# The half q too much in VectorE's rows of an L1-distance attention: taken off through sums of q, or by row matmuls on q itself

## The reference, cut to what matters

```python
def one_query(qs):
    return -jnp.sum(jnp.abs(qs[:, None, :, :] - k), axis=-1) * scale   # scale = 1/sqrt(64)
...
v = (x @ wqv_w.T + wqv_b).reshape(b, t, 3 * h, d)
q, vf, vb = (v[:, :, :h], v[:, :, h:2 * h], v[:, :, 2 * h:])
k = x[:, :, None, :] * wk[None, None]
a = _l1_scores(q, k)
a = jnp.concatenate([a, jnp.zeros((b, 1, t, h), a.dtype)], axis=1)
a = jax.nn.softmax(a, axis=1)[:, :t]
bf = jnp.einsum('bsdh,bshw->bdhw', a, vf)
bb = jnp.einsum('bdsh,bshw->bdhw', a, vb)
o = (bf + bb).sum(axis=2).reshape(b, t, d)
```

## Time and profile before

| | us |
|---|---|
| three runs: median (lowest to highest) | 9558.85 (9547.97 to 9571.28) |
| the profiled execution, its own time | 9557.57 |
| its span, first to last instruction | 9555.7 |
| TensorE matmuls busy | 9349.8 (98%) |
| ScalarE busy | 7738.5 (81%) |
| VectorE busy | 7116.6 (74%) |
| mean granted TensorE clock, share of full speed | 0.974 |

### The profile page before, as it was taken

The page is one execution under the profiler, slowest core; times in us unless marked ns, Lnnn a source line. Parts: engine busy times, 40 slices in busy tenths (PEclk is TensorE's granted clock), DMA queues, the critical chain, the costliest instruction groups (busy, mean ns, idle before and its releaser), DMA issues. The chain is left out here.

```text
span 9555.7 us, 239151 instructions
## 1 busy us (share of the span) xinstructions
PE 9349.8 (98%) x106722; PEld 3919.5 (41%) x106722; DVE 7116.6 (74%) x5441; ACT 7738.5 (81%) x3699; POOL 97.2 (1%) x90
## 2 busy tenths in 40 slices
PE   9689999999999999999999999999999999999989
PEld 5333333333333333333333333333333333333357
DVE  1567777777777777778777777777777777777743
ACT  1158888888888888888888888888888888888833
POOL 0000000000000000000000000000000000000021
PEclk7799999999999999999999999999999999999988
DMA  0231010101000000101000000101010000100000
GB/s 3 97 86 15 2 16 2 15 2 15 2 2 15 2 15 2 15 2 15 2 8 10 2 15 2 15 2 15 2 16 2 2 15 2 15 2 2 2 11 4
DMA packets 135012, 112.14 MB, mean 12 GB/s; under 512 B 111234, under 2 KB 115032, under 8 KB 133829
## 3 DMA queue, kind: packets, MB, share of 16 engines
q1 hardware_dynamic: 133998, 96.81, 5.3%
HBM read 56.55 MB, written 40.22 MB: 10 GB/s over the span
## 5 line engine op out<-in xcount | busy, mean ns | idle before, releaser
L708 ACT ACTIVATE ring<-qx,xs 128x3000 f32<-128x3000 f32 x2624 | 7213.9, 2792 | 992.4 <-PE sc L657 945.1
L657 PE MATMUL sc<-ring,window 128*32 128x375 f32 x96000 | 7822.5, 480 | 1.7 <-DVE ring L776 1.7
L776 DVE TENSOR_SCALAR ring<-qx,xs 128x3000 f32<-128x3000 f32 x3376 | 6133.6, 1837 | 1775.1 <-PE sc L657 1713.2
L657 PEld LDWEIGHTS sc<-ring,window 128*32 128x32 f32 x96000 | 3011.9, 109 | 4463.3 <-issue 4224.5
L743 DVE STREAM_TRANSPOSE ext<-ex 128x768 f32<-128x768 f32 x385 | 374.3, 972 | 0.6
L619 PE MATMUL acc<-ex,vb 128*64 128x375 f32 x1544 | 328.7, 504 | 1.3 <-DVE ex L735 1.3
L631 PEld LDWEIGHTS acc<-ext,vf 128*64 128x64 f32 x4704 | 245.4, 136 | 205.8 <-issue 205.0
L631 PE MATMUL acc<-ext,vf 128*64 128x128 f32 (+1 forms) x4704 | 325.1, 277 | 0.2 <-DVE ext L743 0.2
L693 ACT ACTIVATE ex<-sc 128x750 f32<-128x750 f32 x385 | 298.8, 776 | 6.2 <-PE sc L657 6.2
L1067 ACT ACTIVATE hid<-pu,b1c 128x500 f32<-128x500 f32 x192 | 122.5, 677 | 223.3 <-PE pu L1031 223.2
L735 DVE TENSOR_SCALAR ex<-ex,rz 128x750 f32<-128x750 f32 x385 | 233.9, 608 | 0.6
(11 more groups left out here) (167 smaller groups left out, 1415.0 us busy)
## 6 DMA issues: line engine op xcount, KB each, us to landing
qx<-scratch_qk SPq DMA_DIRECT2D x64, 375.0 KB
scratch_v<-vs SPq DMA_DIRECT2D x38, 480.0 KB, 4.3
scratch_qk<-qs SPq DMA_DIRECT2D x32, 375.0 KB, 2.6
vb<-scratch_v SPq DMA_DIRECT2D x128, 92.0 KB
vf<-scratch_v SPq DMA_DIRECT2D x64, 184.0 KB
scratch_v<-w SPq DMA_DIRECT2D x12, 480.0 KB, 4.4
xs<-scratch_x SPq DMA_DIRECT2D x16, 187.5 KB
vb<-scratch_v SPq DMA_DIRECT2D x128, 1.8 KB
```

The source lines that it names most:

```text
L657: mm = pe.matmul(bank[32 * j:32 * j + 32, h, 0:HALF], window[:, HALF_NH * g + j, ROWS - 1 - i:3 * ROWS - 1 - i], ring[:, slot, j, h * HALF ...
L708: act.activation(flat(ring[:, (HALF * g + k) % RING, :, :]), flat(qx[g][:, :, :]), ACT.Abs, bias=xs[g][:, 1, k:k + 1], scale=0.5).then_inc ...
L776: vec.tensor_scalar(flat(ring[:, (HALF * g + k) % RING, :, :]), flat(qx[g][:, :, :]), xs[g][:, 0, k:k + 1], xs[g][:, 1, k:k + 1], ALU.max, ...
```

## The change: the diff

The sums of q and all that makes them go. `select` becomes 128 x 32 (−0.5 on the first 64 partitions, in the columns of VectorE's rows). A tensor `excess` (128 x 8 x 32) is made once as |wk| times `select`. Each tile is now opened by eight fp32 matmuls `excess` x `qx`, of the form of a row's.

```diff
@@ phase_tokens, first half: the load
-        select32 = sbuf(inner, "select32", [3 * HALF_NH, 128])
+        select = sbuf(ctx, "select", [128, 2 * ROWS])
-                    sp.dma_start(select32[:, :], A["select"]).then_inc(loaded, 16)
+                    sp.dma_start(select[:, :], A["select"]).then_inc(loaded, 16)
-                    vec.tensor_copy(select[:, :], select32[:, :])
@@ phase_tokens, second half: SP
-                    sp.dma_start(wqr[:, :, :], A["wqr"].rearrange("p (c d) -> p c d", c=HP)).then_inc(weights, 16)
-                        if c % 10 == 9 and c // 10 < 3:
-                            k = c // 10
-                            sp.wait_ge(part_act, k + 1)
-                            sp.dma_start(parts[:, k, :], kparts[:, k % 2, :]).then_inc(ks_stored[k], 16)
@@ TensorE
-                    pe.wait_ge(signs_made, 1)
-                    for p in range(HP):
-                        pe.matmul(pv[0][0:D, 0:NH], wqr[:, p, :], signs[:, p, :], start=(p == 0), stop=(p == HP - 1))
-                    for p in range(HP):
-                        mm = pe.matmul(pv[1][0:NH, 0:1], signs[:, p, :], bq[:, p:p + 1], start=(p == 0), stop=(p == HP - 1))
-                    mm.then_inc(signed, 1)
-                    pe.wait_ge(signed_kept, 1)
-                    for k in range(2 * B):
-                        if k >= 2:
-                            pe.wait_ge(ks_kept, k - 1)
-                        pe.matmul(pt[k % 2][0:NH, 0:HALF], wqs[:, :], xt[0:D, k * HALF:(k + 1) * HALF],
-                                  start=True, stop=True).then_inc(ks_sum, 1)
@@ ScalarE
-                    act.wait_ge(ks_kept, 2 * B)
-                    act.copy(kparts[:, 0, :], ks32[:, :]).then_inc(part_act, 1)
-                    ... (two more copies, each behind a subtraction)
@@ VectorE
-                    vec.memset(signs[:, :, :], 0.0)
-                    vec.tensor_copy(diag[0:64, 0:HP * NH:NH + 2], wks[0:64, :])
-                    vec.tensor_copy(diag[64:128, 1:HP * NH:NH + 2], wks[64:128, :]).then_inc(signs_made, 1)
+                    vec.tensor_tensor(excess[:, :, :], wka[:, :].unsqueeze(2).to_broadcast([128, NH, 2 * ROWS]),
+                                      select[:, :].unsqueeze(1).to_broadcast([128, NH, 2 * ROWS]), ALU.mult)
-                    vec.wait_ge(signed, 1)
-                    vec.tensor_copy(bqs[:, :], pv[1][0:NH, 0:1])
-                    link(vec.tensor_copy(wqs[:, :], pv[0][0:D, 0:NH]))
-                    vec.sem_inc(signed_kept, 1)
-                    for k in range(2 * B):
-                        vec.wait_ge(ks_sum, k + 1)
-                        vec.tensor_scalar(ks32[:, k * HALF:(k + 1) * HALF], pt[k % 2][0:NH, 0:HALF], bqs[:, :], None,
-                                          ALU.add).then_inc(ks_kept, 1)
-                        if c in KS_AT:
-                            k = KS_AT.index(c)
-                            vec.wait_ge(part_act, k + 1)
-                            vec.tensor_tensor(ks32[:, :], ks32[:, :], kparts[:, k, :], ALU.subtract).then_inc(part_vec, 1)
@@ phase_attend: SP, once in a pair
-                        sp.dma_start(ksum[g][:, :], scratch_ks[3 * HALF_NH * g:3 * HALF_NH * (g + 1),
-                                                               bass.ds(b * L, L)]).then_inc(pair_in[g], 16)
@@ phase_attend: TensorE, once in a tile
                     for h in range(2):
-                        pe.matmul(bank[:, h, 0:HALF], select[:, :], ksum[g][:, h * HALF:(h + 1) * HALF],
-                                  start=True, stop=False, skip_group_check=True)
+                        for j in range(HALF_NH):
+                            pe.matmul(bank[32 * j:32 * j + 32, h, 0:HALF], excess[:, HALF_NH * g + j, :],
+                                      qx[g][:, j, h * HALF:(h + 1) * HALF], start=True, stop=False, skip_group_check=True)
```

More of the change, by code:

```diff
@@ L80, in build @@
         window = sbuf(whole, "window", [128, NH, WIN])
-        select = sbuf(whole, "select", [3 * HALF_NH, 128], BF16)
-        phase_tokens(nc, A, sbuf, psum, semaphore, hx, oacc, window, select, scratch_x, scratch_qk, scratch_ks, scratch_v)
-        phase_attend(nc, sbuf, psum, semaphore, oacc, window, select, scratch_x, scratch_qk, scratch_ks, scratch_v)
+        excess = sbuf(whole, "excess", [128, NH, 2 * ROWS])
+        phase_tokens(nc, A, sbuf, psum, semaphore, hx, oacc, window, excess, scratch_x, scratch_qk, scratch_v)
+        phase_attend(nc, sbuf, psum, semaphore, oacc, window, excess, scratch_x, scratch_qk, scratch_v)
         phase_feed(nc, A, out, sbuf, psum, semaphore, hx, oacc)
@@ L98, in layernorm, with phase_tokens @@
     link(vec.reciprocal(var[:, :], var[:, :]))
-def phase_tokens(nc, A, sbuf, psum, semaphore, hx, oacc, window, select, scratch_x, scratch_qk, scratch_ks, scratch_v):
+def phase_tokens(nc, A, sbuf, psum, semaphore, hx, oacc, window, excess, scratch_x, scratch_qk, scratch_v):
     with ExitStack() as ctx:
@@ L250, in phase_tokens @@
             wkc = sbuf(inner, "wkc", [128, HP])
[L251 to L255, removed]
             wkd = sbuf(inner, "wkd", [128, NH])
@@ L276, in phase_tokens @@
             xt_vec = semaphore(inner, "xt_vec")
[L277 to L283, removed]
             q_sum = semaphore(inner, "q_sum")
@@ L297, in phase_tokens @@
             v_stored = [semaphore(inner, f"v_stored{k}") for k in range(NVS)]
-            ks_stored = [semaphore(inner, f"ks_stored{k}") for k in range(3)]
             NV = TOK // VCH
             QCRED = 2 * HP + 2
-            KS_AT = (4, 12)
-            NWB = 6
+            NWB = 5
             with nc.Block() as block:
@@ L310, in _ @@
                     sp.dma_start(wkd[:, :], A["wkd"]).then_inc(weights, 16)
-                    sp.dma_start(wqr[:, :, :], A["wqr"].rearrange("p (c d) -> p c d", c=HP)).then_inc(weights, 16)
-                    parts = scratch_ks.rearrange("(h k) t -> h k t", k=3)
                     sp.wait_ge(xt_act, NC // 8)
@@ L337, in _ @@
                         sp.wait_ge(v_stored[k], 16 * len(range(k, NV, NVS)))
-                    for k in range(3):
-                        sp.wait_ge(ks_stored[k], 16)
                 @block.tensor
@@ L511, in _, with phase_attend @@
                                               bv[0:VCH, h * 512:(h + 1) * 512], ALU.add).then_inc(v_made, 1)
-                        if c in KS_AT:
-                            k = KS_AT.index(c)
-                            vec.wait_ge(part_act, k + 1)
-                            vec.tensor_tensor(ks32[:, :], ks32[:, :], kparts[:, k, :], ALU.subtract).then_inc(part_vec, 1)
-def phase_attend(nc, sbuf, psum, semaphore, oacc, window, select, scratch_x, scratch_qk, scratch_ks, scratch_v):
+def phase_attend(nc, sbuf, psum, semaphore, oacc, window, excess, scratch_x, scratch_qk, scratch_v):
     with ExitStack() as ctx:
@@ L523, in phase_attend @@
         xs = [sbuf(ctx, f"xs{k}", [128, 2, HALF]) for k in range(2)]
-        ksum = [sbuf(ctx, f"ksum{k}", [3 * HALF_NH, L], BF16) for k in range(2)]
         vb = [sbuf(ctx, f"vb{k}", [128, NT, D]) for k in range(2)]
@@ L550, in phase_attend @@
         NPAIR = 2 * B
-        NLOADS = 2 + 4 + 4 * HALF_NH + 2 * HALF_NH
+        NLOADS = 1 + 4 + 4 * HALF_NH + 2 * HALF_NH
         NA = made_before(HALF, True)
@@ L1148, in arrange @@
     w, bias, wk = g["L0_attn_wqv_w"], g["L0_attn_wqv_b"], g["L0_attn_wk"]
-    select = np.zeros((HALF_NH, 3, 128), f)
-    for p in range(128):
+    select = np.zeros((128, 2 * ROWS), f)
+    for p in range(2 * ROWS):
         if not on_scalar(p % ROWS):
-            select[p // 32, :, p] = -0.5
+            select[0:D, p] = -0.5
     tri = np.zeros((NE, NE), f)
@@ L1162, in arrange @@
         "w4d": np.concatenate([w4, w4]), "w3b": np.concatenate([w3, b3, b4, b4]),
-        "ident": np.eye(128, dtype=f), "select": select.reshape(3 * HALF_NH, 128),
-        "wqr": w[0:NH * D].reshape(HP, 128, D).transpose(1, 0, 2).reshape(128, HP * D),
+        "ident": np.eye(128, dtype=f), "select": select,
         "wqv": np.concatenate([w.T, w.T]), "bq": bias[0:NH * D].reshape(HP, 128).T, "bv": bias[NH * D:],
```

9 lines of the change are left out of this document (removed).

## The result

The changed kernel takes **9781.85 us** (median of four runs, 9771.43 to 9801.34), against 9553.41 us (9541.66 to 9571.28) for the kernel before in the same comparison: a ratio of 1.024, 95% interval 1.0216 to 1.0263. The profiled execution took 9783.44 us, its span 9781.6 us.

The account below looks back on a forecast made before the run. TensorE was taken to bound the kernel: 270 − 0.7 − 21.9 − 7.0 − 6.9 = +233.5 us on the profiled 9557.57 gives 9791.1, with the runs' median 1.3 us higher: 9792 us, 2.4% slower, range 9775 to 9824.

Parts of the forecast that it names:

- TensorE's time is the kernel's time: Attention tiles: ScalarE and VectorE wait for TensorE, so any change in a tile's TensorE time is paid 384 times.
- The opening, +0.70 us a tile: Start of each tile: eight matmuls add 1.263 us, 0.56 us is removed; times 384, +270 us.
- crossing: Going from ring rows to another sort of matmul and back on TensorE; 0.14 us a tile, expected to go.
- The first tile: First tile's opening fits in the 2.53 us before its first row, so its 0.70 us is not paid: −0.7 us.
- The sums' products, −21.9 us: Between q and values: without these products, values begin at 411.42 instead of 433.31, saving 21.9 us.
- The split, −13.9 us: Among the value chunks: the pauses around two subtractions go, −7.0 and −6.9 us.
- Edits with one answer: Small setup edits (`signs`, its products, the `wqr` load, `select`'s load, one DMA less before each pair): taken as 0.
- Behind the loop's jump: Seven jumps where TensorE stands still, then runs at a lower clock: the new opening there counts 0, ±5 us.
- The makers setting the pace: Rival: ScalarE and VectorE, making ring rows, limit the tile, so the opening costs nothing; 9522 us, 3%.
- the opening reading slower than a row: Rival: three engines reading `qx` slow the opening, up to +1.26 us a tile, up to 10277 us; 3%.
- weight loads in the open: Rival: the opening's 16 loads run ahead of its matmuls, 1.74 us more a tile, 10460 us; 1%.
- The crossing that stays: Rival: the 0.14 us is not due to form and remains, 0.84 us a tile, 9846 us; 9%.

Follow-up runs that it names:

- one number in a hand-written order: Kernel before with product back moved from behind row 2 to behind row 5, right ahead of forward: 9447.81 us, 0.9904 of the kernel before.
- the probes: Openings of other forms: fp32 at 128 columns in the kernel before, 9922.78 us; fp32 on 64 rows in the changed kernel, 9641.57 us.

## Why the prediction was right

- **TensorE's time is the kernel's time.** Right: one opening less or more moves the whole by 1.27 or 1.29 us a tile.
- **The opening, +0.70 us a tile.** Right, 0.708. The added part was taken from the nearest row, a ring row, and measured just that, 1.26 us; reading `qx` or starting the bank costs nothing on top. The removed part had two terms, 0.42 us between two starts and 0.14 us of crossing. Without the second, +324 us and 9846 us would have been forecast, above the range's upper end of 9824, and 64 us too much. The two equations with three and ten rows found it in the trace of before. What they could not tell was what the crossing belongs to, and the forecast took it by argument to be the form; the experiments settled it. The 0.42 us held another 0.10 of crossing, which made no difference here, since the whole opening went.
- **The first tile** hides its opening: right. 538.18 to 540.72 is 2.54 us to the first row, as 2.53 before.
- **The sums' products, −21.9 us.** −19.3 measured: the values follow on q at once, but q itself ended at 414.1 and not at 411.4. The stages ahead, whose work is the same, came later by that much; the first product of q already started 1.5 us later (334.26, 332.77 before).
- **The split, −13.9 us.** −15.3 measured from the first to the last chunk. The values now start without the slow first chunks, and keep 1.71 us a chunk to the end; the stores did not become the bound.
- **Edits with one answer:** nothing of them shows. The first product starts at 9.96 us (10.33 before).
- **Behind the loop's jump** the forecast had 0 ± 5, for the clock. What moved was the idle time ahead of the opening, from 17.4 to 22.1 us over the seven jumps, about the 4.5 us by which the openings' part came out too long. The size is inside the ±5, the reason given is not this one; with the same opening and the sums kept it was 17.5 us, so the new opening is not shown to be the cause.
- **Not foreseen:** the 12.3 us behind the attention. The forecast compared one execution with a median and gave the part behind the attention no scatter of its own, where its profiles differ by up to 47 us. Here that was 12 us, inside the range, and partly luck: it hid the 4.5 us, and without it the spans' difference would have been some 5 us above the forecast, not 8 below.
- **The rivals.** The makers setting the pace (3%) and the opening reading slower than a row (3%) are refuted by the runs with none and with two openings; weight loads in the open (1%) by the opening's 1.26 us. The crossing that stays (9%) is refuted here, and the probes show when it would have been right: had the new opening used 64 rows or 128 columns. The Trainium skill's rule on weight loads (TensorE: Matmul & The Clock Gate, section The mechanism), by which they would have come into the open, does not hold here as the prediction put it: 16 loads of 0.109 us lie within the 1.26 us, though all use the same 128 rows. The same section also lets a load go ahead into a background weight buffer, which would fit. What does bring a load into the open in these traces is a change of tiling.

## What to carry to other kernels

Price a swap of matmuls by array passes and by changes of form around them, not by instruction count or operand size: here eight fp32 matmuls cost 1.26 us against 0.42, and fitting in with the neighbours' form gave back only 0.24 us of crossing. Put matmuls that use the same rows and columns of the array side by side; one number in a hand-written order was worth 1%. And look for what is constant over the loop, and for an engine with slack to add it: the correction belonged neither into 384 bf16 openings nor into 384 fp32 ones.

## What the runs showed of the hardware that was not expected

- A short foreign stretch between matmuls of another tiling costs 0.24 to 0.34 us. At a change of tiling the next weight load starts with its matmul, not 0.31 us ahead of it, and the longer that load (0.106 to 0.186 us), the longer the first group (0.339 to 0.419 us). A change between fp32 and bf16 at the same tiling costs nothing that shows.
- Two row tiles of 64, into two banks, work at the same time: eight fp32 matmuls of 375 columns in 0.79 us with the crossing, 1.26 us on 128 rows.
- Identical code with gaps in it varied by 47 us of some 450 over twelve profiles, with TensorE's mean clock between 0.79 and 0.89 of full speed; in the dense part the median tile of two kernels with the same opening is the same, 23.34 us.
